# A softmax attention whose products and values alternate: three pairs and one and a half steps in turn, maxima in a ring of four single banks

## The reference

```python
# 1: attention with softmax, 8 heads of 8 channels, keys and queries over 1024 positions
q, k, v = proj(Wq, bq), proj(Wk, bk), proj(Wv, bv)
attn = softmax(einsum('bhnd,bhmd->bhnm', q, k) * 8 ** -0.5, axis=-1)
out = einsum('bhnm,bhmd->bhnd', attn, v)
x = group_norm(out @ Wo.T + bo, 8 groups) * gn_w + gn_b + x
# 2: four layers of linear attention (8 heads, no softmax), on layer-normed tokens, with a residual
# 3: a mixture of 8 experts (top 2, renormalised), on layer-normed tokens, with a residual
```

## Time and profile before

| what | us |
|---|---|
| median of 3 runs | 254.62 (254.6 to 254.94) |
| the profiled execution | 254.18 |
| its span, first to last instruction | 252.4 |
| TensorE busy in it | 238.2 (94%) |
| VectorE busy | 194.9 (77%) |
| ScalarE busy | 178.6 (71%) |
| GpSimd busy | 46.4 (18%) |

### The profile page before, as it was taken

How to read it: one execution, slowest core, us unless ns; L and a number is a source line. 1 busy time by engine, 2 the same in 40 slices (tenths; PEclk the granted TensorE clock), 3 DMA queues, 4 the chain that set the end, 5 groups by cost and what they waited for, 6 DMA issues and landing times.

```text
span 252.4 us, 5599 instructions
## 1 busy us (share of the span) xinstructions
PE 238.2 (94%) x2105; PEld 109.6 (43%) x2106; DVE 194.9 (77%) x288; ACT 178.6 (71%) x366; POOL 46.4 (18%) x84
## 2 busy tenths in 40 slices
PE   8999998999999999999999999999989988789994
PEld 7455343333334333334343343333333875458420
DVE  2799788989889898898988989889502683359763
ACT  2736697888888888888888888888898132229610
POOL 7964099010010100101001210010100000000340
PEclk9999999999999999999999999999999999999999
DMA  4025300342112031440200000000000000000002
GB/s 135 0 79 170 94 0 4 84 171 68 40 47 68 23 85 39 100 168 5 95 1 3 1 3 2 4 0 4 1 4 1 3 0 3 0 3 0 1 0 86
DMA packets 6099, 10.06 MB, mean 40 GB/s; under 512 B 2240, under 2 KB 3840, under 8 KB 5944
## 3 DMA queue, kind: packets, MB, share of 16 engines
q1 hardware_dynamic: 6072, 9.70, 13.1%
HBM read 6.84 MB, written 2.62 MB: 37 GB/s over the span
## 4 chain that ended last, share of the span: by engine, by line
PE 79%; DVE 7%; POOL 5%; issue 4%; ACT 3%; DVEq 0%; POOLq 0%; ACTq 0%
PE psum L530 25%; PE psum L437 17%; PE psum L472 15%; PE psum L782 2%; PE psum L503 2%; DVE negmax L1141 2%; POOL qop L832 1%; POOL kop L832 1%; PE psum L382 1%; PE psum L540 1%; PE psum L402 1%; PE psum L691 1%; PE psum L496 1%; POOL early L912 1%; PE psum L414 1%
## 5 line engine op out<-in xcount | busy, mean ns | idle before, releaser
L1141 DVE TENSOR_REDUCE negmax<-psum 128x1 f32<-128x1024 f32 x128 | 155.3, 1224 | 14.9 <-PE psum L437 10.5
L979 ACT ACTIVATE probs<-psum 128x512 f32<-128x512 f32 x232 | 126.0, 598 | 19.9 <-PE psum L472 15.8
L437 PE MATMUL psum<-kop,qop 64*128 64x512 f32 x256 | 92.7, 444 | 0.6 <-DVE negmax L1141 0.3
L472 PE MATMUL psum<-qop,kop 64*128 64x512 f32 x256 | 89.6, 445 | 0.1
L530 PE MATMUL psum<-probs,v_aug 128*32 128x256 f32 x1024 | 80.4, 390 | 1.1
L472 PEld LDWEIGHTS psum<-qop,kop 64*128 64x128 f32 x256 | 37.1, 184 | 26.8 <-ACT probs L979 17.8
L437 PEld LDWEIGHTS psum<-kop,qop 64*128 64x128 f32 x256 | 37.6, 184 | 24.5 <-DVE negmax L1141 13.0
L530 PEld LDWEIGHTS psum<-probs,v_aug 128*32 128x32 f32 x1024 | 21.2, 108 | 42.2 <-ACT probs L979 27.2
L867 POOL TENSOR_TENSOR attn<-o_tok,rden 128x64 f32<-128x64 f32 x15 | 4.4, 297 | 105.5 <-DVE rden L1132 105.5
L931 POOL TENSOR_TENSOR early<-probs,early 128x512 f32<-128x512 f32 x4 | 5.1, 1274 | 50.2 <-ACT probs L1077 50.1
L540 PE MATMUL psum<-cbf_sb 128*128 128x256 bf16 x118 | 14.0, 273 | 0.0
(11 more groups left out here) (185 smaller groups left out, 183.4 us busy)
## 6 DMA issues: line engine op xcount, KB each, us to landing
parts_scratch<-early SPq DMA_DIRECT2D x4, 512.0 KB, 3.4
qop<-parts_scratch SPq DMA_DIRECT2D x28, 64.0 KB
vt_sb<-in_vt SPq DMA_DIRECT2D x1, 1024.0 KB, 4.9
kop<-parts_scratch SPq DMA_DIRECT2D x14, 64.0 KB
kop<-parts_scratch SPq DMA_DIRECT2D x28, 32.0 KB
x_sb<-in_x SPq DMA_DIRECT2D x2, 256.0 KB, 2.8
q_pair<-in_q_pairs SPq DMA_DIRECT2D x1, 512.0 KB, 3.3
qop<-max_row SPq DMA_DIRECT2D x28, 4.0 KB
```

The lines of the kernel that those rows point to most:

```text
L437: last = nc.tensor.matmul(psum[:, 2 * (v % 2) + c, :], qop[at, b * PP + pp, qh * NH + t * P:qh * NH + (t + 1) * P], kop[at, b * PP + pp, c ...
L472: last = nc.tensor.matmul(psum[:, bank, :], kop[at, b * PP + pp, mt * P:(mt + 1) * P], qop[at, b * PP + pp, qh * NH:(qh + 1) * NH], start= ...
L979: last = nc.scalar.activation(probs[:, n % P_RING, h, :], psum[:, bank, :], ACT.Exp, scale=SCALE)
L1141: V.tensor_reduce(negmax[:, i, h * HT + t:h * HT + t + 1], psum[:, bank:bank + 2, :].rearrange("p a n -> p (a n)"), AX_X, ALU.max, negate= ...
```

## The change

1. A **pair counter** p = 4g + i orders TensorE's loop. Values no longer stand at fixed places: after every third pair (`PHASE` = 3, p = 2, 5, 8, ...) `values_until` runs up to a goal of p - 4 half steps (`VALUES_LAG`), that is three half steps each time. A goal doesn't cross the end of a block: there it stops, and the next one has up to five. A step can be cut into two halves of its queries, 128 columns per instruction in place of 256. In the wide steps the values stay at the end of each g.
2. **Transposes** of the maxima and of the output, and the copy of the output, hang on p as well: transposes stand only behind a third pair, ahead of the values. The transpose of block blk's maxima stands behind pair 16 blk - 9, rounded up to a third pair; it stood behind pair 16 blk - 7. The copy is behind the exponential of the pair after which the block's values end, the output's transposes two turns (6 pairs) later.
3. **Maxima by halves.** The products of maxima use the four banks 0 to 3 one at a time: half m waits for m - 3 reductions and raises `slot_full` itself. VectorE reduces 512 columns at a time into `half_max`, and after the 8 steps of a block one minimum of two [128, 8] arrays gives `negmax` (they are negated maxima). GpSimd waits for that (`maxima_done`).
4. **Lead.** `CATCH_UP` = (0, 1): g = 1 also does two further maxima steps, so they are 14 steps ahead, and the wide steps begin at g = 57 (14 steps).

```diff
 TOGETHER = 2
 RUNS = UNITS // TOGETHER
 RUNS_OF = TT // TOGETHER
+PAIRS_OF = 2 * TOGETHER
+PHASE = 3
+VALUES_LAG = 4
+MAX_BANKS = 4
+ROWS_AHEAD = 3
 LEAD = TT + 2
-CATCH_UP = (0,)
+CATCH_UP = (0, 1)
...
+        half_max = sb("half_max", [P, 2, HALVES, 2 * HT])
...
-        def block_of_rows(g):
-
-            blk = (g + 2) // RUNS_OF
-            return blk if (g + 2) % RUNS_OF == 0 and DIRECT <= blk <= LAST else None
-
-        def block_of_output(g):
-
-            blk = (g - 1) // RUNS_OF - 1
-            return blk if (g - 1) % RUNS_OF == 0 and 0 <= blk < LAST else None
+        def ends_phase(p):
+
+            return p % PHASE == PHASE - 1
+
+        def phase_end_from(p):
+
+            return p + (PHASE - 1 - p) % PHASE
+
+        FIRST_WIDE = min(g for g in range(RUNS) if not max_jobs(g))
+        WIDE_PAIR = PAIRS_OF * FIRST_WIDE
+
+        values_goal, block_done = {}, {}
+        goal = 0
+        for p in range(PAIRS_OF * RUNS):
+            wide = p >= WIDE_PAIR
+            if p % PAIRS_OF == PAIRS_OF - 1 if wide else ends_phase(p):
+                block_end = 2 * TT * (goal // (2 * TT) + 1)
+                goal = max(0, min(block_end, 2 * TOGETHER * (p // PAIRS_OF) if wide else p - VALUES_LAG))
+                values_goal[p] = goal
+                if goal == block_end:
+                    block_done[goal // (2 * TT) - 1] = p
+
+        def rows_pair(blk):
+
+            p = PAIRS_OF * (RUNS_OF * blk - ROWS_AHEAD) + PAIRS_OF - 1
+            return p if p >= WIDE_PAIR else phase_end_from(p)
+
+        def rows_within(g):
+
+            return next((blk for blk in range(DIRECT, LAST + 1)
+                         if rows_pair(blk) >= WIDE_PAIR and rows_pair(blk) // PAIRS_OF == g), None)
+
+        def output_pair(blk):
+
+            p = block_done[blk]
+            return p + 2 * (PAIRS_OF if p >= WIDE_PAIR else PHASE)
+
+        def small_jobs(p):
+
+            jobs = []
+            if p == phase_end_from(PAIRS_OF * (RUNS_OF - 1) - 1):
+                jobs.append(("max_r", 1, 0))
+            jobs += [("out_t", blk, 0) for blk in block_done if blk < LAST and output_pair(blk) == p]
+            if p < WIDE_PAIR:
+                jobs += [("max_t", blk, 0) for blk in range(DIRECT, LAST + 1) if rows_pair(blk) == p]
+            return jobs
 
         ST_JOBS = [("max_r", 0, 0)]
         for g in range(RUNS):
-            if max_jobs(g):
-                ST_JOBS += [("scores", u, h) for u, h in scores_of(g)[:TOGETHER]]
-                if block_of_rows(g) is not None:
-                    ST_JOBS.append(("max_t", block_of_rows(g), 0))
-                ST_JOBS += [("scores", u, h) for u, h in scores_of(g)[TOGETHER:]]
-            else:
-                ST_JOBS.append(("unit", TOGETHER * g, 0))
-                if block_of_rows(g) is not None:
-                    ST_JOBS.append(("max_t", block_of_rows(g), 0))
-                ST_JOBS.append(("unit", TOGETHER * g + 1, 0))
+            for i in range(PAIRS_OF):
+                p = PAIRS_OF * g + i
+                if g < FIRST_WIDE:
+                    ST_JOBS.append(("scores", *scores_of(g)[i]))
+                    ST_JOBS += small_jobs(p)
+                elif i % 2:
+                    ST_JOBS.append(("unit", p // 2, 0))
+                    if i == 1 and rows_within(g) is not None:
+                        ST_JOBS.append(("max_t", rows_within(g), 0))
+            if g >= FIRST_WIDE:
+                for p in range(PAIRS_OF * g, PAIRS_OF * (g + 1)):
+                    ST_JOBS += small_jobs(p)
             if g == 0:
                 ST_JOBS += [("qk", hf, 0) for hf in range(HALVES)]
-            if g == RUNS_OF - 2:
-                ST_JOBS.append(("max_r", 1, 0))
-            if block_of_output(g) is not None:
-                ST_JOBS.append(("out_t", block_of_output(g), 0))
         st_index = {job: q for q, job in enumerate(ST_JOBS)}
...
+        copies_behind = {}
+        for blk in range(LAST):
+            g, i = divmod(block_done[blk], PAIRS_OF)
+            job = ("scores", *scores_of(g)[i]) if g < FIRST_WIDE else ("unit", TOGETHER * g + 1, 0)
+            copies_behind[st_index[job]] = blk
...
+                m = HALVES * v + c
+                if m >= MAX_BANKS:
+                    pe.wait_ge(S["slot_free"], m - MAX_BANKS + 1)
                 if c == 0:
-                    if v >= 2:
-                        pe.wait_ge(S["slot_free"], v - 1)
...
-                last = nc.tensor.matmul(psum[:, 2 * (v % 2) + c, :],
+                last = nc.tensor.matmul(psum[:, m % MAX_BANKS, :],
                                         qop[at, b * PP + pp, qh * NH + t * P:qh * NH + (t + 1) * P],
                                         kop[at, b * PP + pp, c * NH:(c + 1) * NH], start=True, stop=True)
-                if c == HALVES - 1:
-                    last.then_inc(S["slot_full"], 1)
+                last.then_inc(S["slot_full"], 1)
...
-                        pe.wait_ge(S["slot_free"], UNITS - (1 - bank // 2))
+                        pe.wait_ge(S["slot_free"], HALVES * UNITS - (2 - bank))
...
-            def values(u):
+            def values(u, first, end):
+
                 blk, mt = divmod(u, TT)
                 b, pp, qh = BLOCKS[blk]
+                n = (end - first) * P
+                at = first * P
                 pe.wait_ge(S["st_done"], max(exp_of(u, h) for h in range(2)) + 1)
                 if mt == 0 and blk:
                     pe.wait_ge(S["o_copied"], blk)
@@ -527,11 +577,39 @@
                 for y in range(2):
                     for h in range(2):
                         j = 2 * y + h
-                        last = nc.tensor.matmul(psum[j * VW:(j + 1) * VW, PV_BANK, 0:QB].rearrange("p (x n) -> p x n", x=2),
+                        last = nc.tensor.matmul(psum[j * VW:(j + 1) * VW, PV_BANK, at:at + n]
+                                                .rearrange("p (x n) -> p x n", x=end - first),
                                                 v_aug[:, mt, b, 2 * pp + h, :],
-                                                probs[:, u % P_RING, h, :].rearrange("p (x y n) -> p x y n", x=2, y=2)[:, :, y, :],
-                                                start=mt == 0, stop=mt == TT - 1, skip_group_check=True)
-                last.then_inc(S["pv_done"], 1)
+                                                probs[:, u % P_RING, h, :].rearrange("p (x y n) -> p x y n", x=2, y=2)[:, first:end, y, :],
+                                                start=mt == 0 and first == 0, stop=mt == TT - 1, skip_group_check=True)
+                if end == 2:
+                    last.then_inc(S["pv_done"], 1)
+
+            half_units = [0]
+
+            def values_until(n):
+
+                while half_units[0] < n:
+                    u, first = divmod(half_units[0], 2)
+                    end = 2 if first or half_units[0] + 2 <= n else 1
+                    values(u, first, end)
+                    half_units[0] += end - first
+
+            def small_work(p):
+
+                for kind, blk, _ in small_jobs(p):
+                    if kind == "max_r":
+                        rows_of_max(blk)
+                    elif kind == "max_t":
+                        maxima_to_rows(blk)
+                    else:
+                        output_to_tokens(blk, st_free((kind, blk, 0))).then_inc(S["st_full"], 1)
+
+            def after_pair(p):
+
+                small_work(p)
+                if p in values_goal:
+                    values_until(values_goal[p])
...
+                p = PAIRS_OF * g
                 if jobs:
                     if g == 0:
                         max_half(jobs[0], 0)
@@ -586,17 +665,17 @@
                     scores(*s[0])
                     if g:
                         max_half(jobs[0], 0)
+                    after_pair(p)
                     scores(*s[1])
                     if g:
                         max_half(jobs[0], 1)
-                    if g:
-                        values(TOGETHER * (g - 1))
-                    if block_of_rows(g) is not None:
-                        maxima_to_rows(block_of_rows(g))
+                    after_pair(p + 1)
                     max_half(jobs[1], 0)
                     scores(*s[2])
+                    after_pair(p + 2)
                     max_half(jobs[1], 1)
                     scores(*s[3])
+                    after_pair(p + 3)
...
+                    for i in range(PAIRS_OF):
+                        after_pair(p + i)
 
             attn_to_channels(0)
-            for u in range(UNITS - TOGETHER, UNITS):
-                values(u)
+            values_until(2 * UNITS)
...
-                pool.wait_ge(S["slot_free"], TT * (blk + 1))
+                pool.wait_ge(S["maxima_done"], blk + 1)
...
-                if n % TOGETHER == 1 and (kind == "unit" or (kind == "scores" and h == 1)):
-                    g = n // TOGETHER
-                    if g >= RUNS_OF and g % RUNS_OF == 0:
```

(24 more changed lines are left out.)

12 lines of the change are left out of this document (1 added, 11 removed).

## The result

The changed kernel takes **258.92 us** (median of 4 runs, 257.83 to 261.05) against 254.61 of the kernel before: ratio 1.018, interval 1.0115 to 1.025. It is slower; the forecast was 248.5 in a range from 246.0 to 254.6. The profiled execution is the slowest of the four, 261.05. Executions in the chip's second, slower state are left out of every ratio and count here.

The account below looks back on a forecast made before the run. The prediction took TensorE's order of instructions to bound the loop. Block 10.58 to 10.05 saves 6.8 us, the start .7, the end costs 1.4: 254.18 becomes 248.1, or 248.5 on the median's scale; range 246.0 to 254.6.

Parts of the forecast that it names:

- the turn: TensorE's loop: three pairs and 1.5 steps of values take 1.70 us, bounds 1.67 and 1.88.
- the third pair: TensorE's loop: a third pair in a run adds .225 us, between .22 and .335.
- rival A: TensorE's loop: third pair costs .335, giving 253.0 us (chance .22), or 255.3 with visible loads in the halves (.06).
- the halves: VectorE's loop: reductions of 512 columns stand .598 us apart, at most .688.
- rival C: VectorE's loop: half reductions don't overlap and cost .688 each, block 11.4, time 265.5 us; chance .12.
- GpSimd's chain: At the start: TensorE waits for GpSimd's split of the third block's maxima until 43.68; step 26 at 45.2, gain .7.
- the sum: Whole kernel: start -.7, loop -6.8, end +1.4 us, from 254.18 to 248.1 for the profiled execution.
- I put .2 on each of the two transposes: 10.05: TensorE's loop: bank waits of .2 us at each transpose, block 10.05; bounds 0 and .5 in all.
- TensorE's 9.65: TensorE's time for a block of the loop, transposes included, before any waits for score banks, in us.
- rival D: Loop: waits for score banks eat the saving, .45 us a block, time 254.3; chance .05.
- the end at + 1.4: Behind the last reduction: two more wide exponential steps cost 1.8 us, about .4 comes back.
- late next, at nearly TensorE's price: Loop: VectorE needs 9.96 us a block, against TensorE's 10.05.

Follow-up runs that it names:

- e1_fill: The changed kernel with five small bfloat16 products on zeros before each of the second catch-up's four maximum products; 256.96 us.
- e6_tail: e3_both with values of the two steps before placed ahead of the last maxima's transpose in the first wide turn; 249.2 us.
- e2_late: The changed kernel with both kinds of transposes placed behind the values of their turn, not ahead; 252.4 us.
- e3_both: The changed kernel with the edits of both e1_fill and e2_late; 250.56 us.
- e12_rings_tail: e6_tail with three single banks for the maxima and four for scores and transposes; 257.43 us.
- e5_lead: The kernel before with only the second catch-up at g = 1 (14 steps ahead), double banks and turns of two pairs kept; 255.76 us.
- e11_rings: The changed kernel, transposes in their place, with three single banks for the maxima and four for scores and transposes; 261.89 us.
- e9_outlate: The changed kernel with only the output's transposes behind the values, the maxima's still ahead of them; 255.49 us.
- e10_best: The same kernel as e6_tail, measured again in six executions; 248.73 us.
- e4_two: The changed kernel with two pairs and one step in a turn, values lag 3 half steps; 261.99 us.

## Why the prediction was wrong

**Right, by the numbers of its steps:** the turn (1.68 to 1.70 for 1.70); the third pair (.23 to .24 behind the second for .225, so rival A falls); the halves, which start .60 apart and last 681 ns, as the spacing of the 512-column row said, so rival C falls, too. The Trainium skill's rule on weight loads (TensorE: Matmul & The Clock Gate, The mechanism) doesn't hold for the third pair: the trace has it a tenth of a microsecond closer than the second, on the same two row groups. GpSimd's chain bounds the start once the clock is kept (its split is taken at 43.69 in e1_fill, 43.68 in the sum; step 26 at 45.25); a lead of two more steps costs 1.95 at the end, forecast 1.8.

**Wrong, first: "I put .2 on each of the two transposes: 10.05".** This is the term that failed. The cause named was right (a transpose needs the bank of the run's own first pair), the size was not, and the bounds of 0 to .5 a block were too narrow. TensorE's 9.65 was measured as 10.60, and by the account of the turns the .95 are .28 at the output's transposes, .63 at the maxima's and .05 elsewhere. Moving both off the third pair gives back .54 (.31 and .23 by the runs), and the block is 10.06, where VectorE takes over. In the sum: 12.75 blocks x .55 = 7.0 of the 13 us by which the profiled execution missed the sum (+6.9 where -6.1 was put). The prediction had this as rival D, at .45 a block, and gave it .05. Its .2 is what its own rows give with ScalarE otherwise free: an exponential starts .5 behind its pair and lasts .6, so a bank is free 1.1 behind the first pair, and the third pair ends .57 + .33 = .9 behind it. But .28 was measured even for the output's. In front of the maxima's, ScalarE still had the output's copy in its queue (at 98.97, between the exponentials), which the sum left out: in the turn at 98.42 the third score product starts .39 behind the second in place of .24, and its maximum product .16 later still. What part of the .63 is the bank, the copy and VectorE's pace wasn't isolated further.

One sum of the prediction is short: rival A's block adds .2 for both transposes where the forecast adds .4. With .4 it is 10.6, no saving at all. A didn't come true, so this moved nothing.

**Wrong, second: nothing was put for the second catch-up's own products.** The prediction moved four products to g = 1 and asked only for their operands. They stand alone there, .6 apart at VectorE's pace, TensorE waits nearly half of 2.5 us, and its granted clock falls to the lower level, for 10.2 us in the profiled execution. The filled gaps (e1_fill) bring back 2.7 us at step 26 in the profiled executions; the medians differ by 2.0 in all. The four executions of the changed kernel have mean clocks of .974, .984, .987 and .987, at times of 261.05, 258.78, 259.07 and 257.83: the longest is the one with the lowest clock.

**Wrong, third: the end at + 1.4.** It is + 4.2. Two more wide steps are 1.95 of it, near the 1.8 forecast. The low clock stage is 1.4: the way is 17.48, and 16.08 in e1_fill, which has the same order there at the upper level. The other .9 are waits, and the .4 that was to come back doesn't: the last half step of a block's values had moved behind the gap, so TensorE has nothing to do while it waits for GpSimd (1.18) and then for the copied output (.46). e6_tail takes 1.1 back by order alone.

VectorE "late next, at nearly TensorE's price" was right, but hidden: only when the transposes no longer wait (e2_late, and e3_both with .985 busy) does it bound the loop.

## What to carry to other kernels

When a run of work grows to the size of its bank ring, everything placed behind the run without a bank of its own becomes the ring's extra job: write down when its bank comes free, with the engine's whole queue in front, and put work that needs no bank in between. Single banks paid here because runs of three don't come in whole double banks. And a ring as large as the run was too small: in 60 us of the loop the weight loads of the maximum products waited 10.0 us for VectorE with three banks of maxima (e12_rings_tail) and 1.8 us with four (e3_both). A catch-up that makes one engine follow another's pace alone belongs where it has other work beside it.

## What the runs showed of the hardware

The granted clock was unexpected. A stretch of 2 to 2.5 us in which TensorE got one product of .34 every .6 us, or two every 1.13 (e5_lead), was followed by the lower level (1.2 GHz), from 31 to 35 us on: for 10.2 us in the kernel after, 6.8 in e11_rings, 3.4 in e2_late, e9_outlate and e5_lead. With five small bfloat16 products on zeros in each gap there was none behind it in the profiled executions of e1_fill, e3_both, e6_tail, e10_best and e12_rings_tail. The fill isn't a full safeguard: the kernel with double banks had a low stage of 6.8 us from 24.2 on, ahead of the filled stretch, and one execution each of e3_both and e10_best came at a mean clock of .98 and .986. Nor does the stretch always cost it: the turns of two (e4_two) had the gaps unfilled and kept the clock in the profiled execution. What sets the 3.4 or the 10.2 us of a low stage wasn't tried, nor why the one at the end of the loop comes in after, e2_late and e9_outlate and not in e1_fill.

Changing over between the products and the values costs about .35 a turn, whatever the turn holds. A turn of two pairs and a step is 1.235: two pairs at .23 and a step at .43 leave .345. One of three pairs and one and a half steps is 1.70: three at .23 and 1.5 at .43 leave .365. The timeline doesn't show the cause. Cutting a step into halves of 128 columns cost nothing that it shows: a visit of 8 instructions of 256 columns and 8 of 128 takes .78 (102.76 to 103.54), and .14 + 1.5 x .43 is .785.
